# Attention rows: where the output product stands, and which PSUM bank it writes

## The reference

```python
x = _layernorm(pair_rep, gamma, beta)
q = (x @ Wq * C ** -0.5).reshape(n, s, s, H, C)      # H = 4 heads of C = 32
k = (x @ Wk).reshape(n, s, s, H, C)
v = (x @ Wv).reshape(n, s, s, H, C)
dpa = einsum('nsqhc,nsvhc->nsqvh', k, q) + 1e9 * (mask - 1)[:, None, :, :, None]
attention = softmax(dpa + (x @ Wb)[:, None], axis=3)
out = einsum('nsqvh,nsvhc->nsqhc', attention, v)
out = out * sigmoid(x @ Wu + bu).reshape(n, s, s, H, C)
out = (out.reshape(n, s, s, H * C) @ Wo + bo) * mask[..., None]
x = x + out                                          # the caller's residual
```

## Time and profile before

| | |
|---|---|
| median of 3 runs | 2528.18 us |
| profiled execution | 2533.66 us, span 2531.9 us |
| mean granted TensorE clock | 0.948 of full speed |
| TensorE busy | 2199.2 us (87%) |
| VectorE busy | 2185.8 us (86%) |
| ScalarE busy | 1763.2 us (70%) |
| GpSimd busy | 2075.4 us (82%) |
| attention rows | 75.2 to 427.4 us of the span |

### The profile page before, as it was taken

The page is one execution under the profiler, slowest core; times in us unless marked ns, Lnnn a source line. Parts: engine busy times, 40 slices in busy tenths (PEclk is TensorE's granted clock), DMA queues, the critical chain, the costliest instruction groups (busy, mean ns, idle before and its releaser), DMA issues. The chain is left out here.

```text
span 2531.9 us, 36914 instructions
## 1 busy us (share of the span) xinstructions
PE 2199.2 (87%) x9081; PEld 1134.5 (45%) x9158; DVE 2185.8 (86%) x2247; ACT 1763.2 (70%) x3999; POOL 2075.4 (82%) x1330
## 2 busy tenths in 40 slices
PE   6899997776898889988999889999899999988798
PEld 6566664463444444444444333333344333333543
DVE  5677777535999999999999999999999999998796
ACT  4799997566878778787788755656555656553487
POOL 4455555204999999999999999999999999999489
PEclk9999998786999999999999999999989999989899
DMA  4000000005677766776676777777777767765022
GB/s 71 14 12 12 12 12 8 1 1 139 214 232 227 225 232 223 236 226 224 228 228 234 234 241 247 239 231 241 237 230 246 241 231 243 237 224 183 13 60 63
DMA packets 192552, 421.07 MB, mean 166 GB/s; under 512 B 66548, under 2 KB 95705, under 8 KB 192474
## 3 DMA queue, kind: packets, MB, share of 16 engines
q1 hardware_dynamic: 190938, 416.01, 52.1%
q10 hardware_dynamic: 1536, 4.20, 0.5%
HBM read 387.63 MB, written 24.12 MB: 163 GB/s over the span
## 5 line engine op out<-in xcount | busy, mean ns | idle before, releaser
L1589 POOL TENSOR_TENSOR s_hc<-s_h,s_cc 128x1024 f32<-128x1024 f32 x512 | 1200.8, 2363 | 61.2 <-PE s_py L1342 45.4
L1342 PE MATMUL s_py<-s_hc,ident 128*128 128x512 f32 x2048 | 991.6, 609 | 14.9 <-DVE s_yo L1635 14.5
L1672 DVE TENSOR_TENSOR_SCAN s_h<-s_dA,s_state,s_pu 128x1024 f32<-128x1024 f32 x330 | 770.3, 2342 | 27.7 <-PE s_pu L1320 4.7
L1342 PEld LDWEIGHTS s_py<-s_hc,ident 128*128 128x128 f32 x2048 | 389.9, 195 | 386.5 <-issue 314.6
L1503 ACT ACTIVATE s_dA<-s_dt,ss_A 128x1024 f32<-128x1024 f32 x352 | 401.6, 1142 | 9.2 <-ACT s_brow L1459 7.8
L1508 ACT ACTIVATE s_pu<-s_dt,ss_A 128x1024 f32<-128x1024 f32 x160 | 178.4, 1115 | 322.5 <-DVE s_h L1672 317.0
L1582 POOL TENSOR_TENSOR s_dbx<-s_dtx,s_bb 128x1024 f32<-128x1024 f32 x160 | 377.8, 2362 | 2.5 <-DVE s_dtx L1627 2.5
L1672 DVE TENSOR_TENSOR_SCAN s_h<-s_pu,s_state,s_dbx 128x1024 f32<-128x1024 f32 x150 | 350.2, 2335 | 21.2 <-ACT s_pu L1508 19.8
L1648 DVE TENSOR_TENSOR s_pu<-s_pu,s_dtx 128x1024 f32<-128x1024 f32 x288 | 349.1, 1212 | 15.8 <-PE s_pu L1329 13.5
L1329 PE MATMUL s_pu<-s_bcs,ss_sel 128*128 128x512 bf16 x499 | 163.5, 398 | 121.4 <-DVE s_h L1672 117.2
L588 POOL TENSOR_TENSOR ar_ex<-ar_ex,ar_rs 128x512 f32<-128x512 f32 x128 | 133.0, 1039 | 158.3 <-DVE ar_rs L537 158.2
(11 more groups left out here) (289 smaller groups left out, 3587.0 us busy)
## 6 DMA issues: line engine op xcount, KB each, us to landing
s_cc<-rows_scratch SPq DMA_DIRECT2D x512, 512.0 KB, 4.6
s_bb<-rows_scratch SPq DMA_DIRECT2D x160, 512.0 KB, 4.9
s_n<-n_scratch SPq DMA_DIRECT2D x64, 258.0 KB, 5.6
y_scratch<-s_yo SPq DMA_DIRECT2D x16, 512.0 KB, 5.4
s_yf<-y_scratch SPq DMA_DIRECT2D x16, 512.0 KB, 5.8
x_tok<-in_x_dram SPq DMA_DIRECT2D x16, 256.0 KB, 4.5
at_xg<-at_xT SPq DMA_DIRECT2D x64, 64.0 KB, 2.1
n_scratch<-ss_turned SPq DMA_DIRECT2D x32, 128.0 KB, 4.2
```

The source lines that it names most:

```text
L1342: ins = nc.tensor.matmul(p_y[:, hf], lhsT=c.ident[:, :], rhs=hc[:, s % RING, hf], start=(s == 0), stop=(s == U - 1))
L1589: nc.gpsimd.tensor_tensor(hc[:, s % RING, :], h[:, s % RING, :], cc[:, s % C_RING, :], ALU.mult).then_inc(read, 1)
L1672: nc.vector.tensor_tensor_scan(out=flow(h[:, s % RING, :]), data0=flow(decays), data1=flow(inputs), initial=begun, op0=ALU.mult, op1=ALU.a ...
```

## The change

The output product `p_y` moves out of the attention product's bank into the unused columns of the score bank of head 0. TensorE issues it directly behind the turning instead of at the end of the step; it now waits until the bias addition of the step's own row has read the score bank (`added`), and for the gate of its own row only. The attention product no longer waits for the x addition; the score product of row r waits for the x addition of row r-6, since that reads the bank which the scores are written to. VectorE adds row r-5 to x behind the gate in the same step, where it added row r-6 at the step's beginning.

```diff
-        o_T, p_y = ps_o[:, 0:128], ps_o[:, 128:128 + D]
+        o_T, p_y = ps_o[:, 0:128], ps_s[:, 0, 128:128 + D]
...
-            def project_output(r, j, next_attended):
-                pe.wait_ge(gated, r + 2 if next_attended else r + 1)
+            def project_output(r, j, scores_read):
+                pe.wait_ge(gated, r + 1)
+                if scores_read is not None:
+                    pe.wait_ge(added, scores_read + 1)
                 need(pe, x_done, r)
                 nc.tensor.matmul(p_y, lhsT=og[:, j % 2, :], rhs=wo[:, :], start=True, stop=True).then_inc(y_made, 1)
...
             def attend(r, j, k):
...
                 need(pe, gated, r)
-                need(pe, x_done, r - 1)
...
             def step(r, j, g, k, has, pair):          # TensorE
                 if has(0):
                     need(pe, added, r)
+                    need(pe, x_done, r - 5)
                     score(r, j, g, k)
                 if has(4):
                     attend(r - 4, j, 1 - k)
                 if has(3):
                     turn(r - 3, (j - 3) % GR)
+                if has(5):
+                    project_output(r - 5, (j - 5) % GR, r if has(0) else None)
                 if has(0):
                     values(r, j, k)
...
-                if has(5):
-                    project_output(r - 5, (j - 5) % GR, has(4))
...
             def step(r, j, g, k, has, pair):          # VectorE
-                if has(6):
-                    add_to_x(r - 6)
                 if has(0):
                     add_bias(r, j)
                 if has(4):
                     apply_gate(r - 4, j, g - 1, 1 - k)
+                if has(5):
+                    add_to_x(r - 5)
                 if has(2):
                     invert_sums(r - 2, (j - 2) % GR)
```

## The result

The changed kernel takes 2559.11 us (2556.98 to 2562.33, 4 runs) against 2529.02 (2527.36 to 2532.20, 4 runs) for the kernel before beside it: ratio 1.0119, 95% interval 1.0101 to 1.0136, or 30.1 us more. The forecast was 2551, 23 us more, in a range of 2533 to 2564.

The account below looks back on a forecast made before the run. A loop through several engines, none full, bounds the kernel. Four rows going from 10.87 to 11.69 us add 25.4 us, the drain saves 2.2: 23 us slower, median 2528.18 to 2551, 8-in-10 range 2533 to 2564.

Parts of the forecast that it names:

- part 2: Output product waits for the newest row's bias addition (start A), starting at A + 0.85; TensorE stalls 0.13 us.
- part 3: x addition behind the gate waits for the output product, starting at A + 1.43; VectorE idles 0.59 us per row.
- part 4: VectorE: reciprocal 0.22 us after x addition, minimum at A + 1.73; k projection waits for q, u for k.
- part 6: Reciprocal 0.7 us later delays GpSimd's division; the turn waits 0.12 more in the row after the short one.
- part 7: Score product waits for row r-6's x addition; covered in projecting rows, the short row takes 2.5 us, before 2.02.
- The loop: Steady attention rows: four rows take 11.69 us against 10.87, 25.4 us more over 31 groups.
- The drain: End of the stage after the last bias addition: 8.7 us against 10.9 before, 2.2 us gained.
- Faster: Rival: the bank wait hides behind TensorE's turning; four rows take 10.55 us, total 2516; chance 0.08.
- No change: Rival: ScalarE's chain stays covered; four rows take 10.93 us, total 2528; chance 0.08.
- Slower by more: Rival: 0.1 us more at both output waits, reciprocal and minimum; four rows 12.1 us, total 2564; chance 0.18.
- The two rules of the Trainium skill: VectorE's pipeline drain would add some 5 us, TensorE's weight loads pulled ahead take 6 off; the sum used neither.

Follow-up runs that it names:

- copies first: Changed kernel with ScalarE's copies of q and k put ahead of the exponentials of their step; 2542.5 us, ratio 1.0055 to the kernel before.
- minimum first: Changed kernel with VectorE's reciprocal and minimum put ahead of the x addition; 2536.0 us, ratio 1.0020 to the kernel before.
- reciprocal first: Changed kernel with only VectorE's reciprocal put ahead of the x addition, minimum still behind it; 2552.0 us, ratio 1.0085 to the kernel before.

## Why the prediction was right, and by how much it was off

- *The bank wait (part 2).* Right: load at A + 0.74, and 0.53 behind the turning's start where the product came 0.49 behind it before; with the 0.10 of exposed load (the products of 0.33 now last 0.43 from the load) that is a stall of 0.14, where 0.13 was forecast.
- *The x addition (part 3).* Right: A + 1.42, idle 0.60 on average where 0.59 was forecast.
- *The reciprocal step (part 4).* 0.20, where 0.22 was taken between 0.08 and 0.28.
- *Minimum, exponentials, copy of q, k projection (part 4).* Right, and shown by the experiments: copies first takes this leg out alone, minimum first takes out all that is late on VectorE.
- *Division and turn (part 6).* Right: in the row after the short one the load came at A + 0.87 instead of 0.74; reciprocal first puts a price on it, 8 us.
- *Score's wait for x (part 7).* Right: the short row is 2.48 long where 2.5 was taken. TensorE stands idle for 0.35 in front of its score product.
- *The loop.* 11.69 forecast; 11.73 and 11.85 in turn, 11.79 on average, 31 groups of 0.93 in place of 0.82: 3.4 us more. The 0.12 in every second group, 1.9 us in all, is the u projection behind the copy of k. Part 4 says that u waits for k, but the sum gives it nothing. The other 0.04 is a difference of two errors: the first three rows take 8.82 where the sum had 8.88, and the last takes 2.91 where it had 2.81. The last row is as long with the minimum first, 2.90, so this 0.1 has nothing to do with the waits for q and k; the bias addition that ends it starts 0.66 behind its score product (308.07, 308.73) and not 0.57. In the last group of the loop, where that bias addition is already one of the rows written out behind it, the row takes 2.82, as reckoned, in both kernels. So the 0.1 goes with the loop; through which instruction was not followed up.
- *The drain.* This term of the sum was wrong, and in sign: 12.6 us from the last bias addition (445.64) to the end where 8.7 was forecast and 10.9 taken before. I followed the last row's chain and left out that its reciprocal stands behind the x additions of older rows. It starts 6.6 behind the last bias addition, where 2.45 + 1.75 = 4.2 was reckoned. From the drain of the changed kernel:

```profile
449.56 0.28 DVE L552 SCALAR_TENSOR_TENSOR x_tok<-ar_pss,at_maskT,x_tok 128x64 f32<-128x64 f32 x1 [1.00 <-PE ar_pss L469]
...
452.05 0.28 DVE L552 SCALAR_TENSOR_TENSOR x_tok<-ar_pss,at_maskT,x_tok 128x64 f32<-128x64 f32 x1 [0.99 <-PE ar_pss L469]
452.25 0.17 DVE L539 RECIPROCAL ar_rs<-ar_tot 128x4 f32<-128x4 f32 x1
...
453.59 1.12 PE L487 MATMUL ar_pst<-ident,ar_ex 128*128 128x128 f32 x4 [0.73 <-POOL ar_ex L590]
```

The first two x additions are 2.49 apart, once round the loop x addition, reciprocal 0.20, division 0.25, turn 1.09, output 0.50, x addition 0.45. Then TensorE, busy 2.12 of 4.5 us, falls to its lower clock of 1.2 GHz, and the last turning takes 1.12 where it was 0.66. Windows of the drain, columns as in the earlier trace rows, clock third from the end:

```profile
449.00:453.50 4.50, 2.12 (x27) 1.31 (x25) 1.31 (x6) 1.76 (x6) 2.66 (x6) 0.93 0.02 4
453.50:458.00 4.50, 3.37 (x18) 2.46 (x18) 0.88 (x4) 0.58 (x1) 0.31 (x2) 0.50 0.00 0
```

So of the 3.9 us by which the drain was mis-sized, 2.4 are the late reciprocal. The other 1.5 come behind it, where 4.5 was forecast and 6.0 measured, at the lower clock for the most part; the last output product also waits there for the x addition of the row before. No run separates these two. With reciprocal and minimum first the drain takes 9.3, at a granted clock of 0.93 in its last 5 us. In all, the stage grew by 30.9 in place of 23.2: the drain is 3.9 of the 7.7 that the forecast was short by, the loop 3.4.

- *The rivals.* "Faster" failed on ScalarE and on the 0.13. "No change" is what the kernel with the minimum first became, within 6 us. "Slower by more": the time lies between its 2564 and the forecast, but not by its mechanism, since the two output waits, the reciprocal and the minimum came at the times reckoned.
- *The two rules of the Trainium skill.* The trace after decides as the trace before did. The reciprocal starts 0.20 after an x addition of 0.28. The sentence that the prediction took from "The DRAIN you can't avoid" in the Trainium skill's "VectorE: DVE Perf Modes" is only the first half of what stands there: the same section adds that a next operation which is not held starts earlier, and the trace agrees with that. And the load of the output product is not pulled past the wait, though TensorE is still turning when it comes.

Open: why the u projection meets the copy of k only in every second group was not tried. The kernel's loop runs over two groups at a time, and the longer one is always the first of the two. And the total is nearer to the forecast than its parts deserve: the 0.06 that the first three rows took less made up for some of the 0.1 in the last.

## What to carry to other kernels

Where each engine works through its list in order, the first question about a moved wait is not how long it is but what now stands behind it: here 0.6 us on VectorE hid under nothing, because the minimum behind it feeds ScalarE, which feeds TensorE's next projection. Put work that others wait for ahead of the instruction that waits; in this kernel that order alone was worth 24 of 30 us. And when two results must share a PSUM bank, look at the step with the least other work on TensorE, here the short row: a wait that a projection covers in three rows stands open in the fourth. The kernel that paired results written together and read together had no such wait and was the fastest.

## What the runs showed of the hardware that was not expected

The x addition starts 0.68 after the load of its output product in the loop (303.17, 303.85), but 0.55 in the rows written out behind it, where the address is fixed (438.76, 439.31). The difference of 0.13 goes with an instruction of VectorE's sequencer that only the loop has; it is 0.08 long and starts between the end of the output product (303.17 + 0.43) and the x addition, at 303.7 as far as the view tells, so after the wait and not during it. By the kernel's text it presumably works out the address of row r from the loop's register:

```profile
L552 DVE SCALAR_TENSOR_TENSOR x_tok<-ar_pss,at_maskT,x_tok x112: 283/284/285, 100.2 to 427.9; 128x64 f32 x111, 128x64 f32<-128x64 f32 x1
L552 DVEq FUSED_REGOPS  x111: 80/80/86, 100.1 to 425.0; - x111
```

(All instructions of line 552 in steady rows: duration in ns as least, median, most, then first and last start.) No such instruction stands in front of the x additions written out behind the loop. By this reading 0.13 of every pass through a waiting x addition goes to it; no kernel with a fixed address in the loop was run.
